# Attention scores in four row groups of the PE array: two heads per group in place of eight heads over all rows

## The chip, the cores and the metric

One core of a Trainium2 chip runs the whole kernel. The metric is device time in microseconds, from the start to the end of one execution. Three executions of the kernel before took 331.69, 332.37 and 332.95 us; the median is 332.37 us. Engines are named as in the profile: PE (matrix multiply), PEld (its weight loads), DVE (vector), ACT (scalar, activation), POOL (GpSimd), SP (the engine that issues most loads).

## The reference

One block of a gated cross-attention model on x of shape (2, 1024, 256), all in fp32, with a context of 77 rows per batch:

```
xn  = layernorm(x)                      # no gain, no bias
Q   = xn @ wq.T + bq                    # 16 heads of 16
K,V = ctx @ wk.T + bk, ctx @ wv.T + bv  # 77 keys per batch
s   = Q_h K_h^T / 4, masked: causal (key > query) and padded keys to -inf
x   = x + tanh(g_x) * (softmax(s) V @ wo.T + bo)
xt  = layernorm(x)
e   = argmax(xt @ Wr + br), gate = max softmax of the same
x   = x + tanh(g_f) * gate * expert_e(layernorm(xt))   # 8 experts, 256 -> 1024 -> 256, relu
```

With 77 keys and 1024 queries the causal mask bites only in the first 128 queries of each batch.

## The kernel before

The 2048 query rows are 16 tiles of 128 rows, 8 per batch. A short start loads and transposes the weights (`weight`, L1257: four 128x128 PE transposes into one PSUM bank, then an ACT copy), projects K for both batches, and builds `Kbd`. For each half m of the 256 model columns, eight heads of 16 columns lie on the 128 partitions, and `Kbd[:, b, m]` is block-diagonal: partition p holds the key values of its own head in that head's 77 columns and zero in the other seven heads' columns, 8 x 77 = 616 columns. DVE makes it for batch 0 (`key_blocks`, L788) and POOL for batch 1 in tile 3 (L410); both multiply by a constant mask of block positions (`bdm`).

A tile then goes through these steps, on the engines named. `query` (L1276): PE projects Q transposed, half m = 0 into bank A and half m = 1 into bank T0; ACT adds the bias and writes `QT` (L505, signal act_Q after each half). `scores(i, m)` (L1285): QT half m is the stationary operand (128 rows x 128 queries), Kbd the moving one, in two matmuls of 308 columns (four heads each), one PSUM bank each; in the first tile of a batch a bf16 matmul with an identity adds the mask bias to each bank. The signal pe_S rises after each half. DVE takes the maximum over each head's 77 keys (`smax`, L795), subtracts it and writes the probabilities' buffer `Pb` (`ssub`, L801); ACT takes exp in place (L513). PE transposes Pb in ten chunks in three groups (`transpose_P`, L1307), ACT copies each group to `PT` (`copy_PT`, L518), and PE multiplies with the block form of V in ten matmuls of 51 columns (`attend`, L1331). DVE divides by the row sums (`norm`), PE transposes the result (`transpose_O`, L1346), ACT copies it to `OT`, PE projects it (`project`, L1356) and DVE adds it to x.

The order of the work on every engine is written out by hand, and tiles overlap in it. In the pass of tile n PE runs: scores(n, 0), transpose_O(n-2), scores(n, 1), project(n-2), transposes of P(n-1) in groups 0 and 1, transposes for the layernorms of tiles n+1 and n-3, group 2 of P(n-1), attend(n-1), query(n+1), and the router's logits (`route`) of tile n-3 (L1434 to L1490). ACT runs: copy of OT(n-2), exp(n, 0), copies of PT(n-1), exp(n, 1), the writes of finished rows, and the two QT halves of tile n+1 (L582 to L614). DVE runs: maximum and subtraction of half 0, maximum of half 1, residual of tile n-2, subtraction of half 1, layernorm statistics, router, norm(n-1) (L1007 to L1055). Engines wait for each other by counting semaphores only.

After the tiles, rows are sorted by expert, written to a scratch tensor, gathered in groups of 128 rows of one expert, and the expert layers run over 16 or more such groups (L1546, L1567). That stage takes about half of the time and is not touched.

Of the kernel before, what the change touches and what calls it, by code (L numbers as in the profile page):

```python
# [10 lines left out]
ALU = mybir.AluOpType  # L11
# [3 lines left out]
B, S, D = 2, 1024, 256  # L15
H, DH = 16, 16
LK = 77
# [11 lines left out]
ROUND = 1.5 * 2.0 ** 30  # L29

CONST_COLS = [
    ("ident", 128), ("bdm", 8), ("causal", LK),
    ("e8", 8), ("before", 64), ("k128", 24), ("upto", 64), ("iota128", 128),
    ("pcol", 1), ("p32", 1), ("t1", NT), ("mhalf", 1),
]
# [23 lines left out]
def flamingo(nc, x, ctx_in, mask, g_x, g_f, wq, bq, wk, bk, wv, bv, wo, bo,  # L59
# [5 lines left out]
    with ExitStack() as ctx:  # L65
# [5 lines left out]
        def sbt(name, shape, dt=F32):  # L71

            return sb(name, shape, dt, tiles_only)
# [30 lines left out]
        bias0 = sbt("bias0", [128, B, LK], BF16)  # L104
        identb = sbt("identb", [128, 128], BF16)
# [6 lines left out]
        QT = sbt("QT", [128, 2, 128])  # L112
# [7 lines left out]
        xh = sbt("xh", [128, 2, D])  # L120
        Lg = sbt("Lg", [128, 2, 4, E])
        oh = sbt("oh", [128, NT, E], BF16)
        Kbd = sbt("Kbd", [128, B, 2, 8 * LK])

        iotab = sbt("iotab", [128, 128], BF16)
        ohr = Pb[:, 0, :].bitcast(BF16)[:, 0:NT * 128].rearrange("p (i r) -> p i r", r=128)
# [13 lines left out]
        wr4 = {n: stage("W1", 512).rearrange("p (k d) -> p k d", k=2) for n in ("wk", "wq", "wv", "wo")}  # L140
# [8 lines left out]
        KT = stage("W2", 2 * LK).rearrange("p (m k) -> p m k", m=2)  # L149
        CV = stage("W2", 2 * B * LK).rearrange("p (k b n) -> p k b n", k=2, b=B)  # L150
        vnat = stage("W2", B * H * 17, LK).rearrange("p (b h w) -> p b h w", b=B, w=17)
        brow = stage("W2", 128, 4)
# [5 lines left out]
        def cv(name):  # L158
            a, b_ = CONST_AT[name]
            return cst[:, a:b_]  # L160

        ident = cv("ident")


        pS = ctx.enter_context(nc.psum_tensor("pS", [128, 4, 512], F32))
# [6 lines left out]
        d = {n: sem(f"d_{n}") for n in LOADS}  # L172
# [26 lines left out]
        bank = {"A": pA[:, :], "B": pB[:, :], "S0": pS[:, 0, :], "S1": pS[:, 2, :], "T0": pT[:, 0, :],  # L199
                "T1": pT[:, 1, :]}  # L200
        pctx = pA[:, 0:320].rearrange("p (k n) -> p k n", k=2)[:, :, 0:B * LK]
        blocks = cv("bdm").unsqueeze(2).broadcast_to([128, 8, LK])
        b96_rows = (slice(0, 128), slice(64, 128), slice(64, 128), slice(96, 128), slice(96, 128))

        nth_high, nth_left = {}, {}
# [120 lines left out]
        def _(e):  # L326
# [50 lines left out]
                e.tensor_tensor(W2p[1][c][:, :], W2s[:, bass.ds(r_expert * 2048 + 512 * c, 512)], W2p[0][c][:, :],  # L377
                                ALU.subtract).then_inc(g["pool_W2l"], 1)

            e.dma_start(brow[0:2, :], bq.rearrange("(k p) -> k p", p=128)).then_inc(d["bq"], 16)  # L380
            e.dma_start(brow[2:4, :], bk.rearrange("(k p) -> k p", p=128)).then_inc(d["bk"], 16)
            e.dma_start(bvb, bv.partition_broadcast(128)).then_inc(d["bv"], 16)
            e.wait_ge(d["cst"], 16)
            rstd1(0)
# [10 lines left out]
            for n in range(NT):  # L395
                if n >= 2:
                    rstd2(n - 2)
                if n == 0:
                    e.wait_ge(d["bo"], 16)
                    e.wait_ge(g["act_tg"], 1)  # L400
                    e.tensor_scalar(bob[:, :], bob[:, :], tg[:, 0:1], None, ALU.mult).then_inc(g["pool_bo"], 1)
                    rstd1(2)
                    e.wait_ge(g["pool_bo"], 1)
                    x_plus_bias(0)
                    x_plus_bias(1)
                    e.tensor_copy(iotab[:, :], cv("iota128")).then_inc(g["pool_iota"], 1)
                    e.memset(pay[:, :, 513:PW], 0.0).then_inc(g["pool_pad"], 1)
                    e.wait_ge(d["up"], 16)
                    e.tensor_copy(upperb[:, :], upper).then_inc(g["pool_up"], 1)
                if n == 3:  # L410
                    for m in range(2):
                        e.wait_ge(g["act_KT"], m + 1)
                        e.tensor_tensor(Kbd[:, 1, m, :].rearrange("p (j k) -> p j k", j=8),
                                        KT[:, m, :].unsqueeze(1).broadcast_to([128, 8, LK]), blocks,
                                        ALU.mult).then_inc(g["pool_Kbd"], 1)
                if n + 3 < NT:
                    rstd1(n + 3)
                if n + 2 < NT:
                    x_plus_bias(n + 2)
                if n == 4:  # L420
                    e.wait_ge(g["pool_pad"], 1)
                if n >= 4:
                    store_row(n - 4)
# [65 lines left out]
        def _(e):  # L489
# [15 lines left out]
            def query(i):  # L505
                for m in range(2):
                    e.wait_ge(g["pe_Q"], 2 * i + m + 1)
                    if i:
                        e.wait_ge(g["pe_S"], 2 * (i - 1) + m + 1)
                    e.activation(QT[:, m, :], (pA, bank["T0"])[m][:, 0:128], ACT.Identity,  # L510
                                 bias=bqc[:, m:m + 1]).then_inc(g["act_Q"], 1)

# [248 lines left out]
        def _(e):  # L761
# [25 lines left out]

            def key_blocks(m):  # L788
                e.wait_ge(g["pe_K"], m + 1)
                e.scalar_tensor_tensor(out=Kbd[:, 0, m, :].rearrange("p (j k) -> p j k", j=8),  # L790
                                       in0=pS[:, 3 * m, 0:LK].unsqueeze(1).broadcast_to([128, 8, LK]),
                                       scalar=bkc[:, m:m + 1], in1=blocks, op0=ALU.add,
                                       op1=ALU.mult).then_inc(g["dve_Kbd"], 1)

            def smax(i, m):  # L795
                e.wait_ge(g["pe_S"], 2 * i + m + 1)
                e.tensor_reduce(mx[:, i % 2, 8 * m:8 * m + 8].rearrange("p (n h) -> p n h", n=2), heads(m), AX.X,  # L797
                                ALU.max).then_inc(g["dve_own"], 1)
                return own.up()
# [447 lines left out]
        def _(e):  # L1247
# [5 lines left out]
            def transpose(o, i):  # L1253
                n = i.shape[0]
                return e.transpose(o, i, ident[0:n, 0:n])  # L1255

            def weight(n, bk_):  # L1257

                e.wait_ge(d[n], 16)
                for k in range(2):  # L1260
                    for m in range(2):
                        t = transpose(bank[bk_][:, 256 * k + 128 * m:256 * k + 128 * m + 128],
                                      wr4[n][:, m, 128 * k:128 * k + 128])
                t.then_inc(g["pe_wT"], 1)

            def transpose_x(i):
# [15 lines left out]
                                     stop=(k == 1))  # L1282
                    t.then_inc(g["pe_Q"], 1)

            def scores(i, m):  # L1285
                b, first = i // TPB, i % TPB == 0
                e.wait_ge(g["act_Q"], 2 * i + m + 1)
                if i:
                    e.wait_ge(g["dve_Sm"], 2 * (i - 1) + m + 1)
                if first and m == 0:  # L1290
                    if b:
                        e.wait_ge(g["pool_Kbd"], 2)
                    else:
                        e.wait_ge(g["pool_id"], 1)
                        e.wait_ge(g["act_KT"], 1)
                    e.wait_ge(g["dve_bias0"], b + 1)
                if i == 0 and m == 1:
                    e.wait_ge(g["act_wT"], 3)
                for n in range(2):
                    o = pS[:, 2 * m + n, 0:308]  # L1300
                    t = e.matmul(o, QT[:, m, :], Kbd[:, b, m, 308 * n:308 * n + 308], start=True, stop=not first)  # L1301
                    if first:
                        t = e.matmul(o.rearrange("p (h k) -> p h k", h=4), identb[:, :],
                                     bias0[:, b, :].unsqueeze(1).broadcast_to([128, 4, LK]), start=False, stop=True)
                t.then_inc(g["pe_S"], 1)

            def transpose_P(i, grp):  # L1307
# [124 lines left out]
            e.wait_ge(g["dve_bcol"], 1)  # L1432
            weight("wv", "S1")
            for n in range(NT):  # L1434
                scores(n, 0)
                if n >= 2:
                    transpose_O(n - 2)
                scores(n, 1)
                if n >= 2:
                    project(n - 2)  # L1440
                if n == 1:
                    e.wait_ge(d["sel"], 16)
# [161 lines left out]
def constants():  # L1604
    import numpy as np
    c = np.zeros((128, CONST_W), np.float32)
    p = np.arange(128)

    def put(name, v):
        a, b_ = CONST_AT[name]  # L1610
        c[:, a:b_] = v
    put("ident", np.eye(128))
    put("bdm", (p[:, None] // 16) == np.arange(8)[None, :])
    bm = np.zeros((128, NC, 3, 17))
    sel = np.zeros((128, NC * 179 + 128), np.float32)
    for ch in range(NC):
        for r in range(128):
            row = 128 * ch + r
            if row < HK:
                bm[r, ch, row // LK - chunk_head(ch), :] = 1  # L1620
                sel[row % LK, row] = 1
    sel[:, NC * 128:NC * 179] = bm.reshape(128, -1)
    sel[:, NC * 179:] = p[:, None] < p[None, :]
    put("causal", np.arange(LK)[None, :] > p[:, None])
    put("e8", np.arange(8)[None, :] / 8)
    put("before", (np.arange(8)[None, :] < np.arange(8)[:, None]).reshape(1, 64))
    put("k128", 128 * np.arange(24)[None, :])
    put("upto", (np.arange(8)[None, :] <= np.arange(8)[:, None]).reshape(1, 64))
    put("iota128", p[None, :])
    put("p32", np.where((p % 32 < 8) & (p // 32 != 1), p % 32, -1)[:, None])  # L1630
    put("pcol", p[:, None])
    put("t1", 128 * np.arange(NT)[None, :])
    put("mhalf", -0.5)
    return c, sel
# [24 lines left out]
```

## Time and profile before

| what | value |
|---|---|
| median of 3 runs | 332.37 us |
| profiled execution, its own time | 332.82 us |
| its span, first to last instruction | 330.9 us |
| mean granted clock of PE | 0.957 of full |
| PE busy | 301.2 us (91%) |
| DVE busy | 212.5 us (64%) |
| ACT busy | 181.8 us (55%) |
| POOL busy | 135.9 us (41%) |
| score matmuls (L1301) | 128 passes, 40.2 us busy |

Busy times count an instruction from its start to its end as the profile models it. Matmuls are pipelined, so on PE the end of one lies behind the start of the next, and sums of durations exceed the time that passes; starts and the pieces of the chain are the safer reading. An fp32 matmul appears as two matmul records, each with its own weight load.

### The profile page before, as it was taken

Reading aid. Unit: us, or ns where it says so; the run is one execution under the profiler, and the core shown is the slowest. Engines: PE = TensorE matmul, PEld = TensorE weight load, DVE = VectorE, ACT = ScalarE, POOL = GpSimd, SP = SyncE. Lnnn points to the kernel's source line nnn. Section 1 sums busy time; section 2 is a strip of 40 time slices with the busy share of each in tenths; the row PEclk is TensorE's granted clock in tenths of the full one; section 3 lists DMA queues with packets and bytes.
Section 4 is the critical chain, followed back from the end, with each engine's and each line's share of the span. In section 5 each row is a group of like instructions: output and inputs, shape, how many; then the busy total and the mean of one; then the engine's idle time right before and its main releaser. Section 6 shows DMA issues by size and latency. Waiting matters only on the chain.

```text
span 330.9 us, 7543 instructions
## 1 busy us (share of the span) xinstructions
PE 301.2 (91%) x2348; PEld 276.5 (84%) x2348; DVE 212.5 (64%) x666; ACT 181.8 (55%) x485; POOL 135.9 (41%) x247
## 2 busy tenths in 40 slices
PE   6899999999999999998456999999999999999960
PEld 2569898889899999988325999999999999999960
DVE  4588789989888887777773774345446653344640
ACT  2325567776666666663425875554358743555540
POOL 2444446544444544422635166332234832332250
PEclk9799999999999999999856999999999999999995
DMA  6999990000004444441214102222112121112100
GB/s 172 274 320 378 374 320 8 32 33 34 33 34 161 160 161 159 162 160 43 89 44 120 33 7 66 67 57 70 56 48 62 34 82 51 62 54 77 53 17 5
DMA packets 19890, 34.52 MB, mean 104 GB/s; under 512 B 2564, under 2 KB 14656, under 8 KB 19845
## 3 DMA queue, kind: packets, MB, share of 16 engines
q1 hardware_dynamic: 15509, 21.29, 19.7%
q0 software_dynamic: 4192, 12.62, 12.3%
q8 instruction: 21, 0.34, 0.4%
q14 instruction: 24, 0.20, 0.2%
q10 hardware_dynamic: 144, 0.07, 0.1%
HBM read 27.61 MB, written 6.88 MB: 104 GB/s over the span
## 4 chain that ended last, share of the span: by engine, by line
PE 73%; DVE 7%; issue 5%; ACT 4%; DMA 3%; POOL 3%; POOLq 1%; SPq 1%; DVEq 0%; ACTq 0%
PE pS L1546 21%; PE pB L1567 15%; PE pS L1301 9%; PE pB L1342 9%; PE pT L1255 5%; PE pA L1255 4%; PE pB L1367 3%; DMA W1s<-in_L_xattn_wq_dram 2%; PE pA L1281 2%; PE pT L1281 1%; DMA zin<-rows_dram,idxg 1%; PE pT L1376 1%; POOL W2p L377 1%; DVE Pb L805 1%; DVE mx L797 1%
## 5 line engine op out<-in xcount | busy, mean ns | idle before, releaser
L1546 PE MATMUL pS<-znf,W1c 128*128 128x128 f32 x672 | 83.9, 280 | 0.0
L1546 PEld LDWEIGHTS pS<-znf,W1c 128*128 128x128 f32 x672 | 80.8, 197 | 0.0
L1567 PE MATMUL pB<-W2p,hT 128*128 128x256 f32 x480 | 62.7, 286 | 0.3
L1567 PEld LDWEIGHTS pB<-W2p,hT 128*128 128x128 f32 x480 | 58.7, 191 | 0.9 <-POOL W2p L377 0.7
L1179 DVE TENSOR_SCALAR hA<-pS,b1s 128x128 f32<-128x128 f32 x84 | 23.7, 344 | 54.6 <-PE pS L1546 31.6
L371 POOL DMA_INDIRECT out_dram<-yo,idxs x20 | 21.5, 1074 | 72.7 <-DVE yo L1193 54.9
L681 ACT ACTIVATE hA<-pS,b1s 128x128 f32<-128x128 f32 x84 | 24.0, 368 | 44.4 <-PE pS L1546 38.6
L1301 PE MATMUL pS<-Kbd,QT 128*128 128x308 f32 x128 | 40.2, 433 | 1.9 <-ACT QT L510 1.0
L1342 PE MATMUL pB<-VB,PT 128*128 128x51 f32 (+1 forms) x320 | 37.3, 272 | 0.0
L1342 PEld LDWEIGHTS pB<-VB,PT 128*128 128x128 f32 (+1 forms) x320 | 37.0, 192 | 0.0
L516 ACT ACTIVATE Pb<-Pb 128x616 f32<-128x616 f32 x32 | 23.2, 724 | 24.2 <-DVE Pb L805 24.2
L797 DVE TENSOR_REDUCE mx<-pS 128x8 f32<-128x616 f32 x32 | 25.4, 794 | 11.1 <-PE pS L1301 10.1
L692 ACT ACTIVATE hT<-hA 128x512 fp32r<-128x512 f32 x42 | 27.1, 645 | 8.1 <-DVE hA L1179 7.7
L365 POOL DMA_INDIRECT zin<-rows_dram,idxg x23 | 23.5, 1020 | 17.4 <-issue 13.3
L1301 PEld LDWEIGHTS pS<-Kbd,QT 128*128 128x128 f32 x128 | 21.7, 190 | 7.5 <-ACT QT L510 2.6
L1186 DVE TENSOR_TENSOR hT<-hA,hT 128x512 fp32r<-128x512 f32 x42 | 27.9, 703 | 0.1
L805 DVE TENSOR_TENSOR Pb<-pS,mx 128x616 f32<-128x616 f32 x32 | 25.4, 795 | 1.9 <-DVE mx L797 0.5
L343 POOL TENSOR_SCALAR mv<-mv 128x1 f32<-128x1 f32 x16 | 3.5, 221 | 53.9 <-DVE mv L833 53.8
L1255 PE MATMUL pT<-cst,Pb 128*128 128x128 f32 (+1 forms) x160 | 23.5, 277 | 0.6 <-DVE Lg L847 0.4
L1255 PEld LDWEIGHTS pT<-cst,Pb 128*128 128x128 f32 (+1 forms) x160 | 17.7, 139 | 3.6 <-issue 0.8
L524 ACT ACTIVATE PT<-pT 128x512 f32<-128x512 f32 x32 | 17.6, 594 | 4.0 <-PE pT L1255 2.9
L673 ACT ACTIVATE znf<-pA,bcol 128x128 f32<-128x128 f32 x44 | 18.1, 477 | 2.0 <-PE pA L1255 2.0
(198 smaller groups left out, 497.1 us busy)
## 6 DMA issues: line engine op xcount, KB each, us to landing
W1s<-in_L_ffn_W_dram SPq DMA_DIRECT2D x8, 1024.0 KB, 9.7
W2s<-in_L_ffn_W_dram SPq DMA_DIRECT2D x8, 1024.0 KB, 11.2
rows_dram<-pay POOLq DMA_DIRECT2D x16, 260.0 KB, 2.6
xs<-in_x_dram SPq DMA_DIRECT2D x3, 512.0 KB, 7.7
W2s<-in_sel_dram SPq DMA_DIRECT2D x1, 385.0 KB
zin<-rows_dram,idxg POOLq DMA_INDIRECT x23, 3.7
out_dram<-yo,idxs POOLq DMA_INDIRECT x20
W1s<-in_L_xattn_wk_dram SPq DMA_DIRECT2D x1, 256.0 KB, 3.2
```

The source lines that it names most:

```text
L365: e.indirect_dma_start(zin[s % NZ][:, :], None, scratch, bass.IndirectOffsetOnAxis(ap=idxg[:, s:s + 1], axis=0)).then_inc(gsem[s % NZ], 16)
L681: e.activation(hA[2 * (s % 2)][:, 128 * c:128 * c + 128], pS[:, 2 * (s % 2), 128 * c:128 * c + 128], ACT.Relu, bias=b1s[:, c, s:s + 1]).th ...
L692: e.activation(hT[s % 2][0][:, 512 * n:512 * n + 512], hA[2 * (s % 2) + n][:, :], ACT.Copy).then_inc(g["act_hT"], 1)
L797: e.tensor_reduce(mx[:, i % 2, 8 * m:8 * m + 8].rearrange("p (n h) -> p n h", n=2), heads(m), AX.X, ALU.max).then_inc(g["dve_own"], 1)
L805: e.tensor_tensor(Pb[:, i % 2, 616 * m:616 * m + 616].rearrange("p (n h k) -> p n h k", n=2, h=4), heads(m), mx[:, i % 2, 8 * m:8 * m + 8] ...
L1179: e.tensor_scalar(hA[2 * (s % 2) + 1][:, 128 * c:128 * c + 128], pS[:, 2 * (s % 2) + 1, 128 * c:128 * c + 128], b1s[:, 4 + c, s:s + 1], 0. ...
L1186: e.tensor_tensor(lo, hA[2 * (s % 2) + n][:, :], hi, ALU.subtract).then_inc(g["dve_hT"], 1)
L1255: return e.transpose(o, i, ident[0:n, 0:n])
L1301: t = e.matmul(o, QT[:, m, :], Kbd[:, b, m, 308 * n:308 * n + 308], start=True, stop=not first)
L1342: t = e.matmul(pB[:, 17 * h0:17 * h0 + 51], PT[0:n, i % 2, c, :], VB[0:n, b, c, :], start=(c == 0), stop=(c == NC - 1), skip_group_check=True)
L1546: t = e.matmul(pS[:, 2 * (s % 2) + n, 128 * c:128 * c + 128], W1c[k][n][:, 128 * c:128 * c + 128], znf[s % 2][:, 128 * k:128 * k + 128], s ...
L1567: t = e.matmul(o, hT[s % 2][a][:, 128 * c:128 * c + 128], W2p[b_][c // 2][:, D * (c % 2):D * (c % 2) + D], start=False, stop=(c == 7 and a ...
```

## The change

The 16 heads are laid out differently, and the scores are computed in 32-row groups of the array. The rows of Q and K are permuted (in the transposes of wq and wk, and in the loads of bq and bk) so that half m holds, in partitions 32r to 32r+31, the two heads 4r + 2m and 4r + 2m + 1. Kbd then needs only 2 x 77 = 154 columns per half: which two heads they are depends on the partition's group. The scores of a tile are eight matmuls of 32 rows x 154 columns, group r writing to PSUM bank r, first the columns of m = 0 and then those of m = 1, so each bank holds four heads in the old order. All eight are one call, with one signal pe_S at its end; it waits for both halves of QT and, for the bank space, for both subtractions of the tile before. In PE's order transpose_O(n-2) and project(n-2) follow that call directly. What DVE and ACT do with the scores keeps its shapes.

```diff
-        Kbd = sbt("Kbd", [128, B, 2, 8 * LK])
+        Kbd = sbt("Kbd", [128, B, 2, 2 * LK])
...
-            e.dma_start(brow[0:2, :], bq.rearrange("(k p) -> k p", p=128)).then_inc(d["bq"], 16)
-            e.dma_start(brow[2:4, :], bk.rearrange("(k p) -> k p", p=128)).then_inc(d["bk"], 16)
+            for lo, v, n in ((0, bq, "bq"), (2, bk, "bk")):
+                e.dma_start(brow[lo:lo + 2, :].rearrange("m (r x) -> m r x", r=4),
+                            v.rearrange("(r m x) -> m r x", r=4, m=2)).then_inc(d[n], 16)
...
                     if i:
-                        e.wait_ge(g["pe_S"], 2 * (i - 1) + m + 1)
+                        e.wait_ge(g["pe_S"], i)
...
             def smax(i, m):
-                e.wait_ge(g["pe_S"], 2 * i + m + 1)
+                e.wait_ge(g["pe_S"], i + 1)
...
                 for k in range(2):
+                    o = bank[bk_][:, 256 * k:256 * k + 256]
+                    by_head = o.rearrange("p (m r x) -> p r m x", m=2, r=4)
                     for m in range(2):
-                        t = transpose(bank[bk_][:, 256 * k + 128 * m:256 * k + 128 * m + 128],
-                                      wr4[n][:, m, 128 * k:128 * k + 128])
+                        t = transpose(by_head[:, 2 * m:2 * m + 2, :, :] if n in ("wq", "wk")
+                                      else o[:, 128 * m:128 * m + 128], wr4[n][:, m, 128 * k:128 * k + 128])
...
-            def scores(i, m):
+            def scores(i):
                 b, first = i // TPB, i % TPB == 0
-                e.wait_ge(g["act_Q"], 2 * i + m + 1)
+                e.wait_ge(g["act_Q"], 2 * i + 2)
                 if i:
-                    e.wait_ge(g["dve_Sm"], 2 * (i - 1) + m + 1)
+                    e.wait_ge(g["dve_Sm"], 2 * i)
...
-                        e.wait_ge(g["act_KT"], 1)
+                        e.wait_ge(g["act_KT"], 2)
+                        e.wait_ge(g["act_wT"], 3)
...
-                for n in range(2):
-                    o = pS[:, 2 * m + n, 0:308]
-                    t = e.matmul(o, QT[:, m, :], Kbd[:, b, m, 308 * n:308 * n + 308], start=True, stop=not first)
-                    if first:
-                        t = e.matmul(o.rearrange("p (h k) -> p h k", h=4), identb[:, :],
-                                     bias0[:, b, :].unsqueeze(1).broadcast_to([128, 4, LK]), start=False, stop=True)
+                for m in range(2):
+                    for r in range(4):
+                        rows = slice(32 * r, 32 * r + 32)
+                        t = e.matmul(pS[:, r, 154 * m:154 * m + 154], QT[rows, m, :], Kbd[rows, b, m, :],
+                                     start=(m == 0), stop=(m == 1 and not first), skip_group_check=True)
+                if first:
+                    for r in range(4):
+                        t = e.matmul(pS[:, r, 0:308].rearrange("p (h k) -> p h k", h=4), identb[:, :],
+                                     bias0[:, b, :].unsqueeze(1).broadcast_to([128, 4, LK]), start=False, stop=True,
+                                     skip_group_check=True)
                 t.then_inc(g["pe_S"], 1)
...
             for n in range(NT):
-                scores(n, 0)
+                scores(n)
                 if n >= 2:
                     transpose_O(n - 2)
-                scores(n, 1)
-                if n >= 2:
                     project(n - 2)
```

## Rows read from the trace of the kernel before

**Rows 1.** Busy time by stretch: us, then PE, PEld, DVE, ACT, POOL (instructions), clock, DMA
```profile
91.90:141.70 49.80, 49.80 (x362) 44.97 (x362) 41.00 (x129) 32.25 (x86) 23.17 (x57) 1.00 0.40 139
```
**Rows 2.** The page's chain that ended last, by line, shares of the span
```profile
PE pS L1546 21%; PE pB L1567 15%; PE pS L1301 9%; PE pB L1342 9%; PE pT L1255 5%; PE pA L1255 4%; PE pB L1367 3%; DMA W1s<-in_L_xattn_wq_dram 2%; PE pA L1281 2%; PE pT L1281 1%; DMA zin<-rows_dram,idxg 1%; PE pT L1376 1%; POOL W2p L377 1%; DVE Pb L805 1%; DVE mx L797 1%
```
**Rows 3.** The chain in order of time, tile 11: start us, us, what
```profile
109.81 0.22 PE pA L1255 x2
110.03 1.04 PE pS L1301 x4
111.07 0.86 PE pB L1367 x4
...
113.49 2.17 PE pB L1342 x20
```
**Rows 4.** Timeline of PE, tile 11: start us, us, engine line op out<-in xcount
```profile
108.53 1.28 PE L1301 MATMUL pS<-Kbd,QT 128*128 128x308 f32 x4
109.65 0.38 PE L1255 MATMUL pA<-cst,On 128*128 128x128 f32 x2
...
110.90 1.03 PE L1367 MATMUL pB<-woT,OT 128*128 128x256 f32 x4
111.77 1.04 PE L1255 MATMUL pT<-cst,Pb 128*128 128x128 f32 x8
...
116.82 0.76 PE L1301 MATMUL pS<-Kbd,QT 128*128 128x308 f32 x2
```
**Rows 5.** Timeline of ACT, then of DVE, tile 11
```profile
108.36 0.37 ACT L510 ACTIVATE QT<-pT,bcol 128x128 f32<-128x128 f32 x1
110.06 0.39 ACT L534 ACTIVATE OT<-pA 128x256 f32<-128x256 f32 x1 [1.33 <-PE pA L1255]
111.58 0.72 ACT L516 ACTIVATE Pb<-Pb 128x616 f32<-128x616 f32 x1 [1.13 <-DVE Pb L805]
112.40 1.09 ACT L524 ACTIVATE PT<-pT 128x512 f32<-128x512 f32 x2
...
109.85 0.80 DVE L797 TENSOR_REDUCE mx<-pS 128x8 f32<-128x616 f32 x1 [0.68 <-PE pS L1301]
110.75 0.80 DVE L805 TENSOR_TENSOR Pb<-pS,mx 128x616 f32<-128x616 f32 x1
```
**Rows 6.** Timeline, tile 15
```profile
145.12 0.72 ACT L516 ACTIVATE Pb<-Pb 128x616 f32<-128x616 f32 x1 [1.49 <-DVE Pb L805]
...
145.75 1.07 ACT L524 ACTIVATE PT<-pT 128x512 f32<-128x512 f32 x2
...
146.38 0.44 PE L1255 MATMUL pT<-cst,Pb 128*128 128x128 f32 x2 [0.17 <-ACT PT L524]
```
**Rows 7.** Timeline of ACT, then of PE, start of tile 6
```profile
65.26 0.37 ACT L510 ACTIVATE QT<-pA,bcol 128x128 f32<-128x128 f32 x1
...
65.68 1.30 PE L1301 MATMUL pS<-Kbd,QT 128*128 128x308 f32 x4 [0.54 <-ACT QT L510]
```
**Rows 8.** Timeline of PE after the last tile: transpose and projection with nothing between
```profile
153.69 0.40 PE L1255 MATMUL pA<-cst,On 128*128 128x128 f32 x2
...
154.56 1.13 PE L1367 MATMUL pS<-woT,OT 128*128 128x256 f32 x4 [0.47 <-ACT OT L534]
```
**Rows 9.** Timeline of the start and of tiles 0 and 1
```profile
8.99 1.11 PE L1255 MATMUL pT<-cst,W1s 128*128 128x128 f32 x4 [2.60 <-DMA W1s<-in_L_xattn_wq_dram]
...
13.09 1.63 DVE L790 SCALAR_TENSOR_TENSOR Kbd<-pS,bcol,cst 128x616 f32<-128x616 f32 x2 [0.89 <-PE pS L1427]
...
14.98 0.59 ACT L502 ACTIVATE W1s<-pS 128x512 f32<-128x512 f32 x1
15.55 0.76 PE L1301 MATMUL pS<-Kbd,QT 128*128 128x308 f32 x2 [0.74 <-DVE bias L785]
17.29 0.80 DVE L797 TENSOR_REDUCE mx<-pS 128x8 f32<-128x616 f32 x1
...
24.09 0.78 DVE L797 TENSOR_REDUCE mx<-pS 128x8 f32<-128x616 f32 x1
```

More of the change, by code:

```diff
@@ L31 @@
 CONST_COLS = [
-    ("ident", 128), ("bdm", 8), ("causal", LK),
+    ("ident", 128), ("pair", 2), ("causal", LK),
     ("e8", 8), ("before", 64), ("k128", 24), ("upto", 64), ("iota128", 128),
@@ L201, in flamingo @@
         pctx = pA[:, 0:320].rearrange("p (k n) -> p k n", k=2)[:, :, 0:B * LK]
-        blocks = cv("bdm").unsqueeze(2).broadcast_to([128, 8, LK])
+        pairs = cv("pair").unsqueeze(2).broadcast_to([128, 2, LK])
         b96_rows = (slice(0, 128), slice(64, 128), slice(64, 128), slice(96, 128), slice(96, 128))
@@ L412, in _ @@
                         e.wait_ge(g["act_KT"], m + 1)
-                        e.tensor_tensor(Kbd[:, 1, m, :].rearrange("p (j k) -> p j k", j=8),
-                                        KT[:, m, :].unsqueeze(1).broadcast_to([128, 8, LK]), blocks,
+                        e.tensor_tensor(Kbd[:, 1, m, :].rearrange("p (j k) -> p j k", j=2),
+                                        KT[:, m, :].unsqueeze(1).broadcast_to([128, 2, LK]), pairs,
                                         ALU.mult).then_inc(g["pool_Kbd"], 1)
@@ L789, in key_blocks @@
                 e.wait_ge(g["pe_K"], m + 1)
-                e.scalar_tensor_tensor(out=Kbd[:, 0, m, :].rearrange("p (j k) -> p j k", j=8),
-                                       in0=pS[:, 3 * m, 0:LK].unsqueeze(1).broadcast_to([128, 8, LK]),
-                                       scalar=bkc[:, m:m + 1], in1=blocks, op0=ALU.add,
+                e.scalar_tensor_tensor(out=Kbd[:, 0, m, :].rearrange("p (j k) -> p j k", j=2),
+                                       in0=pS[:, 3 * m, 0:LK].unsqueeze(1).broadcast_to([128, 2, LK]),
+                                       scalar=bkc[:, m:m + 1], in1=pairs, op0=ALU.add,
                                        op1=ALU.mult).then_inc(g["dve_Kbd"], 1)
             def smax(i, m):
-                e.wait_ge(g["pe_S"], 2 * i + m + 1)
+                e.wait_ge(g["pe_S"], i + 1)
                 e.tensor_reduce(mx[:, i % 2, 8 * m:8 * m + 8].rearrange("p (n h) -> p n h", n=2), heads(m), AX.X,
@@ L1283, in query @@
                     t.then_inc(g["pe_Q"], 1)
-            def scores(i, m):
+            def scores(i):
                 b, first = i // TPB, i % TPB == 0
-                e.wait_ge(g["act_Q"], 2 * i + m + 1)
+                e.wait_ge(g["act_Q"], 2 * i + 2)
                 if i:
-                    e.wait_ge(g["dve_Sm"], 2 * (i - 1) + m + 1)
-                if first and m == 0:
+                    e.wait_ge(g["dve_Sm"], 2 * i)
+                if first:
                     if b:
@@ L1294, in scores @@
                         e.wait_ge(g["pool_id"], 1)
-                        e.wait_ge(g["act_KT"], 1)
+                        e.wait_ge(g["act_KT"], 2)
+                        e.wait_ge(g["act_wT"], 3)
                     e.wait_ge(g["dve_bias0"], b + 1)
-                if i == 0 and m == 1:
-                    e.wait_ge(g["act_wT"], 3)
-                for n in range(2):
-                    o = pS[:, 2 * m + n, 0:308]
-                    t = e.matmul(o, QT[:, m, :], Kbd[:, b, m, 308 * n:308 * n + 308], start=True, stop=not first)
-                    if first:
-                        t = e.matmul(o.rearrange("p (h k) -> p h k", h=4), identb[:, :],
-                                     bias0[:, b, :].unsqueeze(1).broadcast_to([128, 4, LK]), start=False, stop=True)
+                for m in range(2):
[3 more added lines that the diff above has]
+                                     start=(m == 0), stop=(m == 1 and not first), skip_group_check=True)
+                if first:
+                    for r in range(4):
+                        t = e.matmul(pS[:, r, 0:308].rearrange("p (h k) -> p h k", h=4), identb[:, :],
+                                     bias0[:, b, :].unsqueeze(1).broadcast_to([128, 4, LK]), start=False, stop=True,
+                                     skip_group_check=True)
                 t.then_inc(g["pe_S"], 1)
@@ L1612, in constants @@
     put("ident", np.eye(128))
-    put("bdm", (p[:, None] // 16) == np.arange(8)[None, :])
+    put("pair", (p[:, None] % 32 // 16) == np.arange(2)[None, :])
     bm = np.zeros((128, NC, 3, 17))
```

## The prediction

> **What bounds the kernel now.** I read the busy shares by stage first. From 91.9 to 141.7 us PE is busy 49.80 of 49.80 us and DVE 41.00 [rows 1]. The chain that ended last gives the score line L1301 9% of the span; the largest shares, L1546 and L1567, are the expert layers, which this change doesn't touch [rows 2]. So the score matmuls are on the path. Next the chain in order of time for tile 11: the pieces are all PE's, one after another. The first score call takes 1.12 us (108.53 to the transposes at 109.65) and the second 1.04, in a period of 8.29 (108.53 to 116.82) [rows 3, 4]. So PE is the bound from tile 9 on.
>
> Then I asked how much air the other engines have, because a shorter PE helps only until the next chain is late. That chain goes round as well: scores, DVE maximum (L797) and subtraction (L805), ACT exp (L516), and only behind the exp, in ACT's order, the copy of the transposed probabilities (L524) for which PE waits before its last transposes and L1342. In tile 11: score start 108.53, maximum 109.85, subtraction 110.75, exp 111.58, copy 112.40 [rows 4, 5]. The exp was not what the copy waited for there: in tile 15 the copy starts 0.63 us after the exp (145.12, 145.75), in tile 11 0.82 after, so this chain has 0.19 us of air in 3.87. Tile 15 also shows what happens when the air is gone: copy at 145.75, PE starts its last transposes at 146.38 with "ACT PT L524" as releaser [rows 6]. In tile 6, with more on ACT, the score matmul itself waits for QT from ACT (65.68) [rows 7]. Two chains are nearly equally long, and the change shortens one of them and may lengthen the other.
>
> **The change, part by part.**
>
> *Column time of the scores: nothing saved in itself.* Each fp32 matmul shows as two passes, each with a weight load. Before, 4 matmuls of 308 columns are 8 passes; 1.04 us for 4 of them is 0.26 each [rows 3]. L1367 gives the same per column (0.86 us for 4 passes of 256). After, 8 matmuls of 154 columns are 16 passes of 0.13: again 2.08 us. Weight loads double, from 8 to 16. L1342 gives their price where the moving side is short: 20 passes of 51 columns in 2.17 us, 0.109 each [rows 3]. All gain must come from row groups working at once, of which no row here has an example. I call the PE time of a tile's scores X and bound it:
> - nothing at once: 16 x 0.13 = 2.08;
> - loads one after another, matmuls overlapped: 16 x 0.109 + 0.13 = 1.87;
> - both overlapped, matmuls starting in program order. The order is r0 first pass, r0 second pass, r1 first pass, ... The two passes of one group share its rows and can't overlap, while the second pass of one group can lie beside the first of the next: 8 x 0.13 + 0.13 = 1.17;
> - all four groups free of each other: 4 rounds x 0.13 = 0.52.
>
> I take 1.17. Loads already run ahead of matmuls here (0.109 under a 0.26 pass), so I expect overlap, but two passes behind each other in one group block the queue.
>
> The Trainium skill bears on this twice. "TensorE: Matmul & The Clock Gate", Part 3, says four row tiles start about 4 ns apart, which would put X near 0.55, the last bound. The same part says matmuls start and end strictly in program order, which leads to 1.17 for this order of passes. No run here shows either. "TensorEngine Tiling (Array Packing)", Key Properties, says a change of tiling mode drains the engine; by that the transposes behind the scores would start later, by up to the 0.24 us by which four passes outlast their 4 x 0.26 (1.28 shown at 108.53 [rows 4]).
>
> *Both halves of Q first.* The scores now wait for act_Q of both halves. In tile 11 the second QT ends 108.36 + 0.37 = 108.73 [rows 5]; a score starts about 0.05 after its QT (tile 6: 65.26 + 0.37 = 65.63, score 65.68 [rows 7]). So 108.78 in place of 108.53: +0.25. Behind this wait on PE stand transpose_O, project and the transposes of the probabilities. The other waits, dve_Sm of the tile before and pe_S before overwriting QT, were met long ago.
>
> *One signal in place of two.* DVE's first maximum waited for half of the scores and now waits for all. Before, it began 1.32 us after the score start, 0.29 more than the 4 x 0.26 of PE time. After, 0.25 + X + 0.29. The rest of that chain keeps its shapes: 0.90 to the subtraction, 0.83 to the exp, at least 0.63 to the copy. The copy starts at 0.25 + X + 0.29 + 2.36 = 2.90 + X, against 3.87 before. **A tile changes by X - 0.97**: +0.20 at X = 1.17.
>
> *The cover of transpose_O's copy is gone.* The second score call stood between transpose_O and project. Before: transpose 109.65, OT copy 110.06 (0.39), project 110.90, never late. Where nothing covers it the tail shows the price: transpose 153.69, project 154.56, PE idle with "ACT OT L534" as releaser: 0.87 for two transposes that take 0.22, so 0.65 us of new idle [rows 3 to 5, 8]. On PE the copy of the probabilities may then start at 0.25 + X + 0.87 + 0.87 (project) + 0.63 (transposes to copy, 111.77 to 112.40) = 2.62 + X. That is 0.28 earlier than by DVE's chain, so the gap is hidden behind DVE and ACT, and a drain under 0.28 with it. Without that cover the gap would cost its 0.65 per tile.
>
> *Start.* Kbd on DVE shrinks from 616 to 154 columns twice: most of 1.63 us at 13.09, off the path. The scores also wait for ACT's third weight copy, 14.98 + 0.59 = 15.57; an earlier Kbd lets ACT's first KT begin up to 0.5 earlier, but QT and wv bound that, so I give it 0.1: score start 15.5, as before (15.55). The first maximum, at 17.29, then waits for all: 15.5 + 1.17 + four bias passes at 0.13 + 0.1 for their first load + 0.29 = 17.58, +0.3. DVE is the path there, so it counts. In tile 1 the maximum at 24.09 follows with no idle time before it, so DVE was late there and not the scores, and nothing changes [rows 9]. The strided outputs of the wq and wk transposes: wk's lie before wq arrives (8.99); wq's 1.11 us is on the path, so between 0 and +0.5 if the strides halve their rate; I take 0, since only the order within the row changes. The bias loads on POOL's queue are cut into eight pieces each in place of two; PE transposes them ahead of wq, and at 8.99 it had waited 2.60 us for wq, so up to that a later landing is covered [rows 9]. Kbd on POOL for the second batch shrinks, and POOL is 23.17 of 49.80 us busy [rows 1].
>
> *Sum.* Tiles 2 to 15: 14 x 0.20 = 2.8. Tile 0: 0.3. Together +3.1 us. The profiled execution took 332.82 (span 330.9 and 1.9 around it) and gives 335.9; the median, 332.37, lies 0.45 under it and gives 335.5. Uncertain inside this case: X by 0.1 (1.4 us), waits by 0.05 a tile (0.7), wq's transposes 0.5, so 333 to 338.
>
> **The rivals.** "Same" is within 0.5%, 1.7 us, about what this kernel's measurement can tell from no change.
> - *Groups wholly independent (faster).* X = 0.52: 14 x (0.52 - 0.97) = -6.3, tile 0 -0.35: 325.7. It decides the sign from X = 0.97 down. PE by its own waits would be at 2.62 + 0.52 = 3.14, DVE's chain at 3.42, so nothing else catches the gain. For: four banks and four groups don't touch each other. Against: the two passes per group stand together in the order.
> - *Loads don't overlap.* X = 1.87: 14 x 0.90 = 12.6, tile 0 +1.0: 346.0. For: L1342 runs at exactly the load's pace, never faster. Against: those loads all fill the same rows.
> - *It doesn't do what it says.* The groups run one after another, X = 2.08: 14 x 1.11 = 15.5, tile 0 +1.2: 349.1. For: no row shows groups at once.
>
> **How the numbers follow.** Program-order overlap 0.36, independent groups 0.28, loads in series 0.25, nothing at once 0.11. Likeliest: 335.5, its own range 333 to 338. The range 326 to 348 takes in the first rival but its last 0.3 us and the second with 2 us of air, and leaves most of the third out. Faster: 0.26 of the independent case and 0.02 of the likeliest, 0.28. Within: 0.02 and 0.07, 0.09. Slower: 0.27 + 0.25 + 0.11 = 0.63.
>
> **What the profile after would show.** Score starts 8.5 us apart in tiles 9 to 14 (8.29 before), 7.9 for the first rival, 9.2 and 9.4 for the others. Score starts sitting behind the second QT. The first maximum 1.17 + 0.29 after the score start. PE idle about 0.65 before project with OT as releaser, and before the last transposes with PT as releaser. I am wrong if the first maximum comes less than 1.2 us after the score start (the groups are freer than the order allows), if PE never waits for PT (the DVE chain is not the bound), or if transpose_O starts more than 0.28 late after the last score pass (the drain decides).

## The result: faster, by about one per cent

The changed kernel took 328.63 us (median of 4 runs, 326.49 to 331.83) beside 332.42 before: ratio 0.9855, interval 0.9826 to 0.9883. Timed once more beside the kernel before, it took 329.83 against 332.58 (medians): ratio 0.9891, interval 0.9855 to 0.9926. Runs at the slow end of its scatter, one in each series, are left out of the ratios, and not of the medians. The forecast was 335.5, slower. The time lay inside its range, on the other side of no change.

The chain that ended last, changed kernel, by engine and by line (before: [rows 2]). The score line, now L1306, falls from 9% to 3%, and ACT and DVE have 20% of the chain (11% before):

```profile
PE 61%; DVE 11%; ACT 9%; issue 7%; DMA 3%; POOL 3%; POOLq 1%; SPq 1%; DVEq 0%; ACTq 0%
PE pS L1552 22%; PE pB L1573 15%; PE pB L1350 6%; PE pA L1257 4%; PE pT L1257 4%; PE pS L1306 3%; PE pB L1375 3%; DVE mx L799 2%; DVE Pb L807 2%; DMA cst<-in_consts_dram 2%; ACT QT L512 2%; DMA zin<-rows_dram,idxg 1%; ACT PT L526 1%; PE pA L1285 1%; ACT Pb L518 1%
```

Timeline of PE, tile 11 (before: [rows 4]). Score starts are 7.92 us apart (8.29 before), and PE idles 0.47 us before project:

```profile
106.80 0.81 PE L1306 MATMUL pS<-Kbd,QT 32*128 32x154 f32 x16
107.53 0.44 PE L1257 MATMUL pA<-cst,On 128*128 128x128 f32 x2
108.45 1.13 PE L1375 MATMUL pB<-woT,OT 128*128 128x256 f32 x4 [0.47 <-ACT OT L536]
109.42 1.04 PE L1257 MATMUL pT<-cst,Pb 128*128 128x128 f32 x8
...
114.72 0.81 PE L1306 MATMUL pS<-Kbd,QT 32*128 32x154 f32 x16
```

ACT and DVE in the same tile (before: [rows 5]):

```profile
106.38 0.37 ACT L512 ACTIVATE QT<-pT,bcol 128x128 f32<-128x128 f32 x1
108.01 0.38 ACT L536 ACTIVATE OT<-pA 128x256 f32<-128x256 f32 x1 [1.27 <-PE pA L1257]
109.41 0.72 ACT L518 ACTIVATE Pb<-Pb 128x616 f32<-128x616 f32 x1 [1.01 <-DVE Pb L807]
110.05 1.08 ACT L526 ACTIVATE PT<-pT 128x512 f32<-128x512 f32 x2
...
107.67 0.80 DVE L799 TENSOR_REDUCE mx<-pS 128x8 f32<-128x616 f32 x1 [0.32 <-PE pS L1306]
108.58 0.80 DVE L807 TENSOR_TENSOR Pb<-pS,mx 128x616 f32<-128x616 f32 x1
```

Sixteen passes last 0.81 us from the first start to the last end, and the first maximum comes 0.87 after the start. Taking off the 0.29 that the prediction put between PE's time and the maximum, X is 0.58. A stretch of 0.02 us at the start of the same call, PE and its loads, shows four passes and four loads under way together:

```profile
106.80 0.41 PE L1306 MATMUL pS<-Kbd,QT 32*128 32x154 f32 x4
106.80 0.20 PEld L1306 LDWEIGHTS pS<-Kbd,QT 32*128 32x128 f32 x4 [0.20 <-ACT QT L512]
```

Where the time went, by stage: from tile 2's score start to tile 15's it took 105.49 us (33.02 to 138.51) against 109.98 (31.73 to 141.71), so -4.5. From tile 0's score start to tile 2's it took 17.50 against 16.18, so +1.3. From tile 15's score start to the first expert matmul (L1546, now L1552) 35.98 against 36.26, so -0.3. Together -3.5. The profiled runs differ by 5.0 (332.82, 327.83); the other 1.5 lies behind the start of the last expert matmul, 9.5 us to the end against 11.0. That is not the row groups' doing: with them and without, this stretch took 9.4 to 9.6 us in ten of the profiles and 10.9 to 11.3 in four (9.5 with the full rows of the first experiment, 10.9 with the row groups and the fill below). The +1.3 is new, in rows of the changed kernel (start of the program, PE, then the clock as the third figure from the right):

```profile
21.58 0.81 PE L1306 MATMUL pS<-Kbd,QT 32*128 32x154 f32 x16 [0.29 <-ACT QT L512]
24.03 1.33 PE L1454 MATMUL pT<-W2s 77*128 77x102 f32 x10 [1.64 <-DVE bcol L1053]
25.20 2.02 PE L1454 MATMUL pB<-W2s 77*128 77x102 f32 x10
...
33.02 0.81 PE L1306 MATMUL pS<-Kbd,QT 32*128 32x154 f32 x16
...
138.51 0.81 PE L1306 MATMUL pS<-Kbd,QT 32*128 32x154 f32 x16
```
```profile
24.00:27.00 3.00, 2.97 (x20) 3.00 (x21) 2.69 (x4) 0.72 (x1) 2.39 (x7) 0.76 1.09 363
27.00:29.00 2.00, 2.00 (x12) 2.00 (x11) 1.72 (x4) 0.64 (x2) 0.00 (x0) 0.51 1.04 404
```

The same in the kernel before:

```profile
24.32 1.33 PE L1448 MATMUL pT<-W2s 77*128 77x102 f32 x10 [0.37 <-DVE bcol L1051]
25.48 1.28 PE L1448 MATMUL pB<-W2s 77*128 77x102 f32 x10
...
31.73 1.20 PE L1301 MATMUL pS<-Kbd,QT 128*128 128x308 f32 x4
...
141.71 1.28 PE L1301 MATMUL pS<-Kbd,QT 128*128 128x308 f32 x4
```
```profile
27.00:29.00 2.00, 2.00 (x19) 1.75 (x17) 1.92 (x7) 1.76 (x6) 0.00 (x0) 1.00 1.01 388
```

The shorter score call leaves PE idle for 1.64 us in tile 1, where it waits for DVE (0.37 before), and then the granted clock goes to its lower level, 1.2 GHz. Ten matmuls of one shape take 2.02 us just after ten of the same shape took 1.33; before, 1.33 and 1.28. Before, the clock was 1.00 in both stretches.

### The profile page after: what moved, and what is told of

It reads as the page before. It is cut to its first block, busy times and chain, and to the rows that moved or that the text cites. A ratio compares the mean times of both kernels' runs of the same rounds, so it can differ in the third digit from the quotient of the medians.

```text
span 325.8 us, 7783 instructions
## 1 busy us (share of the span) xinstructions
PE 285.8 (88%) x2476; PEld 264.3 (81%) x2476; DVE 211.3 (65%) x666; ACT 180.7 (55%) x485; POOL 134.3 (41%) x247
## 4 chain that ended last, share of the span: by engine, by line
PE 61%; DVE 11%; ACT 9%; issue 7%; DMA 3%; POOL 3%; POOLq 1%; SPq 1%; DVEq 0%; ACTq 0%
PE pS L1552 22%; PE pB L1573 15%; PE pB L1350 6%; PE pA L1257 4%; PE pT L1257 4%; PE pS L1306 3%; PE pB L1375 3%; DVE mx L799 2%; DVE Pb L807 2%; DMA cst<-in_consts_dram 2%; ACT QT L512 2%; DMA zin<-rows_dram,idxg 1%; ACT PT L526 1%; PE pA L1285 1%; ACT Pb L518 1%
## 5 line engine op out<-in xcount | busy, mean ns | idle before, releaser
L1552 PE MATMUL pS<-znf,W1c 128*128 128x128 f32 x672 | 83.8, 279 | 0.0
L1552 PEld LDWEIGHTS pS<-znf,W1c 128*128 128x128 f32 x672 | 80.7, 197 | 0.0
L1257 PE MATMUL pT<-cst,Pb 128*128 128x128 f32 (+1 forms) x160 | 24.2, 284 | 0.8 <-DVE Lg L849 0.4
L1375 PE MATMUL pB<-woT,OT 128*128 128x256 f32 x56 | 15.8, 405 | 6.6 <-ACT OT L536 6.6
L1257 PEld LDWEIGHTS pT<-cst,Pb 128*128 128x128 f32 (+1 forms) x160 | 18.6, 144 | 3.6 <-ACT PT L526 0.9
L1375 PEld LDWEIGHTS pB<-woT,OT 128*128 128x128 f32 x56 | 9.5, 189 | 10.7 <-ACT OT L536 10.0
## 6 DMA issues: line engine op xcount, KB each, us to landing
W2s<-in_L_ffn_W_dram SPq DMA_DIRECT2D x8, 1024.0 KB, 11.3
```

The lines of the kernel that those rows point to most:

```text
L1375: t = e.matmul(pr_bank(i), OT[:, k, :], wT["wo"][:, k, :], start=(k == 0), stop=(k == 1))
L1552: t = e.matmul(pS[:, 2 * (s % 2) + n, 128 * c:128 * c + 128], W1c[k][n][:, 128 * c:128 * c + 128], znf[s % 2][:, 128 * k:128 * k + 128], s ...
```

## The experiments

**The price of the merged call.** Full 128-row matmuls as before, with the changed kernel's order, waits and single signal (shown against the changed kernel, in part):

```diff
-                        t = e.matmul(pS[:, r, 154 * m:154 * m + 154], QT[rows, m, :], Kbd[rows, b, m, :], ...
+                        t = e.matmul(o, QT[:, m, :], Kbd[:, b, m, 308 * n:308 * n + 308], ...
```

> The kernel before with its full 128-row score matmuls (8 passes of 308 columns, 2.08 us of PE time), but with the order, the waits and the one signal of the changed kernel. It prices the reorder alone. The prediction's rule (period 8.29 + X - 0.97, the way through DVE and ACT) gives score starts 9.4 us apart in tiles 9 to 14 and about 349 us. Rival: PE's own way alone counts (scores, idle before project, project, transposes): 9.1 apart and about 345 us. Second rival: the order costs nothing, 8.3 to 8.5 apart and 332 to 335 us.

349.68 us, ratio 1.0485 (1.0442 to 1.0528), score starts 9.40 apart. The prediction's rule gave 9.40 and 349. So the reorder costs 1.1 us a tile at X = 2.08. Of the two ways to the copy the one through DVE and ACT ends last, but only by 0.10 us, as the rows show: the copy starts 0.62 behind the exp, and the transposes that it copies, 0.63 ahead of it in other tiles, started 0.73 ahead here:

```profile
111.50 2.34 PE L1301 MATMUL pS<-Kbd,QT 128*128 128x308 f32 x8
113.88 0.80 DVE L797 TENSOR_REDUCE mx<-pS 128x8 f32<-128x616 f32 x1 [1.97 <-PE pS L1301]
...
115.50 1.04 PE L1255 MATMUL pT<-cst,Pb 128*128 128x128 f32 x8
115.61 0.72 ACT L516 ACTIVATE Pb<-Pb 128x616 f32<-128x616 f32 x1 [1.14 <-DVE Pb L805]
...
116.23 1.07 ACT L524 ACTIVATE PT<-pT 128x512 f32<-128x512 f32 x2
```

**Does program order hold a group back?**

```diff
-                for m in range(2):
-                    for r in range(4):
+                for r in range(4):
+                    for m in range(2):
```

> The same eight score matmuls, issued group by group (both halves of group 0, then of group 1, ...) in place of half by half. After the change the 16 passes of a tile took 0.58 us of PE time, four at once. Theory A (each row group works off its own matmuls, whatever stands before them in program order): the same 0.81 us from the first score pass to the end of the last, score starts 7.92 us apart in tiles 9 to 14. Rival B (a matmul may not start before the one ahead of it has started, and the half-by-half order is what hid that): two matmuls of one group block the next group, starts at 0, 0.26, 0.26, 0.52, ... 1.04, so 1.30 us of PE time, 1.5 us first to last, score starts 8.5 to 8.7 apart. Rival C (B for single passes): 1.7 us of PE time, score starts about 9.0 apart.

0.83 us, 7.95 apart: theory A. For matmuls of different groups it made no difference which of the two orders they stood in.

```profile
109.45 0.83 PE L1306 MATMUL pS<-Kbd,QT 32*128 32x154 f32 x16
117.40 0.83 PE L1306 MATMUL pS<-Kbd,QT 32*128 32x154 f32 x16
```

**Is it the distinct groups?**

```diff
-                        rows = slice(32 * r, 32 * r + 32)
+                        rows = slice(0, 32)
```

> The changed kernel with all eight score matmuls of a tile reading rows 0 to 31 (QT and Kbd of group 0; the scores of the other groups' heads are left out, group 0's stand in their place). Same count, same shapes, same banks, but one row group. If distinct row groups are what lets four passes run at once: the 16 passes follow each other, 16 x 0.13 = 2.08 us of PE time, about 2.3 from first start to last end, score starts 9.4 us apart in tiles 9 to 14. Rival: the narrow form is cheap in itself (32 rows, or distinct banks): 0.8 us as before and 7.9 apart.

2.36 us from first to last: one group works in series, and narrowness alone gives nothing. From tile 3 on its tiles are 9.5 to 12.5 us apart and the kernel takes 386.09 us, more than the rule says: the granted clock fell again and again though PE was busy (stretch from 90 us: 45.34 of 48 us, clock 0.78):

```profile
109.34 2.36 PE L1306 MATMUL pS<-Kbd,QT 32*128 32x154 f32 x16
90.00:138.00 48.00, 45.34 (x278) 40.87 (x277) 30.36 (x93) 24.49 (x63) 16.41 (x40) 0.78 0.13 45
```

With two groups, by turns (`rows = slice(32 * (r % 2), 32 * (r % 2) + 32)`):

> As e9_one_group, with groups 0 and 1 by turns (groups 2 and 3 left out, 0 and 1 in their place). If each group works off its own passes: 8 x 0.13 = 1.04 us of PE time, 1.25 to 1.35 from first start to last end; the rule 8.29 + X - 0.97 gives 8.4 us from score to score. Rival: four at once or none, then 0.8 or 2.3 us.

1.32 us, and 8.44 apart where the clock was up (8.4 forecast); 10.1 in the tiles where it fell (0.93 over the stretch). So 2.36, 1.32, 0.81 for one, two and four groups: the time halves with each doubling, but for 0.3 us that stays.

```profile
98.58 1.32 PE L1306 MATMUL pS<-Kbd,QT 32*128 32x154 f32 x16
107.02 1.32 PE L1306 MATMUL pS<-Kbd,QT 32*128 32x154 f32 x16
```

**What sets the pace after the change?** In tile 11 the copy at 110.05 is ready by two ways at once: through DVE and ACT, exp at 109.41 and 0.64 on; through PE, transposes at 109.42 and 0.63 on. To tell whether both bind, one move on PE and one on ACT, each alone and both:

```diff
+                if n:
+                    transpose_P(n - 1, 0)          # PE: ahead of project
                 if n >= 2:
                     project(n - 2)
...
-                    transpose_P(n - 1, 0)          # PE: behind project
...
+                if n:
+                    copy_PT(n - 1, 0)              # ACT: ahead of exp
                 exp(n, 0)
...
-                    copy_PT(n - 1, 0)              # ACT: behind exp
```

> The move on PE alone (first four transposes of P(n-1) before project), ACT's order as in the changed kernel. If DVE and ACT's way binds by itself: score starts 7.9 us apart in tiles 9 to 14, as without the move. If PE's way alone was the bound: 7.4 to 7.6.

> The move on ACT alone (copy of the first P(n-1) chunks before exp(n, 0)), PE's order as in the changed kernel. If PE's way binds by itself: 7.9 us apart in tiles 9 to 14. If DVE and ACT's way alone was the bound: 7.4 to 7.6.

> The changed kernel with two moves: PE transposes the first four chunks of P(n-1) between transpose_O(n-2) and project(n-2), where PE waits 0.47 us for OT, and ACT copies them before exp(n, 0) and not behind it. After the change two ways to that copy are equally long: through PE (scores, idle, project, transposes: 3.25 us from the score start) and through DVE and ACT (maximum, subtraction, exp: 3.25). Theory: both bind, and with both moved the period falls from 7.92 to about 7.4 us in tiles 9 to 14 (PE's work plus the rest of the two waits), 5 to 7 us less than the changed kernel in all. Rival: another engine (DVE, 41.2 of 47.6 us busy there) is the bound as well, and the period stays above 7.8.

7.89, 7.95 (from tile 10 on) and, from tile 10 on, 7.58 (7.92 without a move). In these tiles neither alone does anything, both together take 0.34 off, a little less than expected. With PE's move alone PE waits for the copy, which stands behind the exp; with ACT's move alone the copy waits for PE (a row of each):

```profile
106.33 0.44 PE L1257 MATMUL pT<-cst,Pb 128*128 128x128 f32 x2 [0.22 <-ACT PT L526]
```
```profile
116.48 0.60 ACT L526 ACTIVATE PT<-pT 128x512 f32<-128x512 f32 x1 [1.66 <-PE pT L1258]
```

From tile 3 to tile 10 ACT's move alone makes the tiles longer, 8.5 to 9.2 us in place of 7.9 to 8.7, and its one run took 333.08. With both moves the first transposes fill PE's wait for OT, and the copy no longer stands behind the exp:

```profile
110.88 0.81 PE L1307 MATMUL pS<-Kbd,QT 32*128 32x154 f32 x16
111.62 0.44 PE L1258 MATMUL pA<-cst,On 128*128 128x128 f32 x2
111.89 0.60 PE L1258 MATMUL pT<-cst,Pb 128*128 128x128 f32 x4
112.09 0.38 ACT L536 ACTIVATE OT<-pA 128x256 f32<-128x256 f32 x1 [1.26 <-PE pA L1258]
112.53 1.13 PE L1376 MATMUL pB<-woT,OT 128*128 128x256 f32 x4
112.53 0.60 ACT L526 ACTIVATE PT<-pT 128x512 f32<-128x512 f32 x1
...
113.50 0.72 ACT L518 ACTIVATE Pb<-Pb 128x616 f32<-128x616 f32 x1 [0.37 <-DVE Pb L808]
```

The whole time with both is no better all the same (329.51, ratio 0.9885, 0.9853 to 0.9916). From tile 3's score start to tile 9's, where the scores of either kernel wait for QT from ACT, the moves gain 0.6 us, from tile 9's to tile 15's 1.8; and in the profile tile 0 to tile 2 took 21.45 us (17.50 in the changed kernel's first profile), with the clock down past 33 us. The same two moves on the kernel before:

> The kernel before (full-row scores in two calls) with the two moves of e4_probs_ahead. Theory: before the change PE's own work sets the period in tiles 9 to 14 and has no gap before project, so the moves give nothing there: 8.25 to 8.3 us from score to score; the room that the moves used was made by the row groups. Rival: the copy's order was a bound of the kernel before as well, then 8.0 or less.

8.26: next to nothing. The row groups made the room.

**The wait for the second half of Q.**

```diff
-                e.wait_ge(g["act_Q"], 2 * i + 2)
+                e.wait_ge(g["act_Q"], 2 * i + 1)
...
                 for m in range(2):
+                    e.wait_ge(g["act_Q"], 2 * i + m + 1)
                     for r in range(4):
```

> The changed kernel, with the four matmuls of half 0 waiting for the first QT only, and those of half 1 for the second. If the wait for the second QT is on the path, as forecast at +0.25 us a tile, the first maximum comes 0.15 to 0.25 earlier behind the second QT, score to score 7.7 us in tiles 9 to 14 in place of 7.92, and 2 to 3.5 us less in all. Rival: that wait is hidden (the time is set by another way round), then 7.92 stays and the time is that of the changed kernel.

7.75 apart from tile 10 on. The wait was on the path, worth 0.17 of the 0.25 forecast. The second half shows no wait of its own: the 16 passes take 0.81 us as without the split. The scores now follow PE's matmuls for the router's logits (L1385) at once, so PE's own order sets their start:

```profile
112.73 0.51 PE L1385 MATMUL pT<-wrs,XX 128*128 128x8 f32 x4
112.93 0.37 ACT L512 ACTIVATE QT<-pT,bcol 128x128 f32<-128x128 f32 x1
113.17 0.81 PE L1307 MATMUL pS<-Kbd,QT 32*128 32x154 f32 x16
```

In the whole time a gain over the changed kernel is not shown: its six runs lie between 324.45 and 331.93, with a median of 330.42. In the profiled one, the longest of them, the clock was still at 0.50 from 29 to 33 us.

**The clock at the start.**

```diff
                 if n == 1:
+                    warm(7, bank["T1"])
                     e.wait_ge(d["sel"], 16)
```

> The changed kernel with seven bf16 matmuls of ones (about 1.5 us, into a free PSUM bank) between the scores of tile 1 and what follows. There the changed kernel left PE idle 1.64 us and the granted clock read 0.51 from 27 to 29 us (1.00 before the change). Theory: the idle time brings the clock down and this costs 1.3 to 1.5 us at the start; then the clock is 1.00 from 24 to 29 us, tile 2's scores start near 31.6 us in place of 33.02, and the ratio to the kernel before falls by about 0.004. Rival: the clock falls for another reason (the 32-row matmuls count for less), then it reads about 0.5 there as well and nothing is gained.

The clock stays at 1.00 from 24 to 29 us, and tile 0 to tile 2 takes 16.11 us (17.50 without, 16.18 before the change):

```profile
27.00:29.00 2.00, 2.00 (x19) 1.71 (x18) 1.97 (x5) 1.39 (x4) 0.15 (x1) 1.00 1.05 400
16.18 0.81 PE L1306 MATMUL pS<-Kbd,QT 32*128 32x154 f32 x16 [0.93 <-ACT W1s L504]
32.29 0.81 PE L1306 MATMUL pS<-Kbd,QT 32*128 32x154 f32 x16
```

So filling the idle time keeps the clock up. That the idle time alone brings it down is not shown, since the fill adds full-row matmuls as well. The rival (32-row matmuls count for less) is not ruled out either: with all scores in one row group (the third experiment) PE had no wait for DVE in tile 1, and the clock fell all the same, while with full rows in one call (the first), where the scores of tile 1 start at 23.90 in place of 23.86 and last 2.34 in place of 2.36, it stayed up. Full rows, then one group:

```profile
27.00:29.00 2.00, 2.00 (x21) 2.00 (x19) 1.97 (x4) 0.72 (x1) 1.71 (x5) 1.00 1.04 407
```
```profile
27.00:29.00 2.00, 2.00 (x14) 2.00 (x13) 1.97 (x4) 0.72 (x1) 1.67 (x4) 0.61 1.02 389
```

So the clock can fall there without that wait, where few rows are at work; whether the wait alone is enough, with full-row scores, was not run. In the whole time (327.5, ratio 0.9836, 0.9801 to 0.9871) the gain of the fill is within the intervals' overlap and not shown. The unaltered changed kernel, timed once more:

> The changed kernel once more, unaltered, timed beside the kernel before. Theory: PE's idle time in tile 1 brings the clock down there in every run, for a length that varies, so the runs scatter by 3 to 5 us (326 to 332) where the kernel before scatters by 2; the fast ones lie near 328, and the clock reads about 0.5 after 25 us in the profile. Rival: the low clock at the start was an accident of single runs, then 1.00 there.

It scattered from 327.63 to 333.22 (the kernel before from 331.76 to 333.96), and the clock was down again, for longer; tile 0 to tile 2 took 19.05 us:

```profile
27.00:29.00 2.00, 2.00 (x12) 2.00 (x11) 1.06 (x2) 0.41 (x1) 0.72 (x2) 0.50 1.02 396
16.75 0.81 PE L1306 MATMUL pS<-Kbd,QT 32*128 32x154 f32 x16 [0.92 <-ACT W1s L504]
35.80 0.81 PE L1306 MATMUL pS<-Kbd,QT 32*128 32x154 f32 x16
```

The clock fell there in all seven profiles of four-group kernels without the fill (the changed kernel twice, and five versions of it), and stayed up in the two with it and in the three with full-row scores.

**All of it together:** the two moves, the split wait and the fill.

> The two moves, the split wait for Q and the fill of PE's idle time in tile 1, all on the changed kernel. If the gains are on one way round they add: period 7.1 to 7.3 us in tiles 9 to 14 and 1.4 us at the start, 317 to 321 us. If DVE becomes the bound: 7.3 to 7.5, and 321 to 324 us.

323.84 us, ratio 0.9709 (0.9681 to 0.9736), 7.4 us apart in tiles 10 to 14. It beats both kernels, and is slower than 317 to 321. The time is that of the second case, but its cause is not: in tiles 11 and 12 (103 to 118 us) every piece of the chain that ended last is PE's but for short issue times, and none is DVE's. Its shares there by line:

```profile
by line: PE pB L1352 31.3%; PE pB L1377 15.1%; PE pT L1258 14.6%; PE pA L1258 10.7%; PE pS L1308 9.8%; PE pA L1286 6.8%; PE pT L1286 6.0%; PE pT L1386 5.4%; issue 0.5%
```

Against the changed kernel's first profile it gains 1.6 us from tile 0 to tile 2 and 2.6 from tile 9 to tile 15, but only 1.2 from tile 3 to tile 9.

## Why the prediction was wrong

- *Column time, the choice of X.* This step failed. It took program-order overlap, X = 1.17; the trace shows 0.58, near the 0.52 of the rival "groups wholly independent". The argument was that the two passes of one group block the queue; the group-by-group order shows that they don't. Four row groups work off their passes at once: from first start to last end 0.81 us with four, 1.32 with two, 2.36 with one. The loads, of which the prediction had feared 0.109 each in series, run four at once. The Trainium skill, "TensorE: Matmul & The Clock Gate", Part 3, has both rules that were weighed: row tiles starting some 4 ns apart agrees with four starts within 0.02 us here; strict program order of starts and ends would have made the group-by-group call longer, and 0.83 us for it speaks against that across groups.
- *The rule, a tile changes by X - 0.97.* Right. At X = 2.08 it gave 9.40, measured 9.40; for two groups 8.4, measured 8.44; at 0.58 it gives 7.90, measured 7.92. With X right the prediction's own sum gives 326.6, near the rival's 325.7, where 328.63 and 329.83 were measured.
- *Both halves of Q:* forecast +0.25. QT ends at 106.75 and the scores start at 106.80. Splitting the wait gave back 0.17, and then PE's own order sets the start. Right in kind, and nearly in size.
- *The cover of OT's copy.* The idle time came, 0.47 us with OT as releaser. It was forecast to hide with 0.28 to spare; the spare was zero, since transpose to project and project to transposes took 0.92 and 0.97 where 0.87 each was reckoned, and the transposes behind the scores started 0.15 late, less than the 0.28 at which the prediction would have put it down to a drain. PE never waited for PT in tiles 9 to 14, one of the signs of being wrong; yet the way through DVE and ACT was no shorter, since moving transposes into the gap was worth something only together with the move on ACT. So both ways bind.
- *Start.* Mis-sized: +0.3 for tile 0 and nothing for tile 1. The first maximum of tile 0 came at 17.00, where 17.58 was forecast: with 0.58 for X the same sum gives 16.99. The maximum in tile 1 did wait for DVE and not for the scores, as said. But PE then stood idle, and tile 0 to tile 2 took 1.3 us more than before in the first profile and 2.9 in the second, with the clock down; the prediction has no term for the clock. Beside the 4.5 that the tiles gain, that is a third in the one and two thirds in the other.
- *Rivals.* Loads in series (346.0) and nothing at once (349.1) are ruled out by X. The independent case had a chance of 0.28 where program order had 0.36; its 325.7 lacks the time lost at the start.

## What to carry to other kernels

Four row groups on four banks cut the PE time of these 32-row matmuls to nearly a quarter (2.08 to 0.58 us), in both orders of issue that were tried; whether it takes four banks was not tried. What the kernel gains is only what the next chain leaves, here 0.37 of 1.5 us a tile. When one call replaces two, price the cover that the second one gave and the signal that the first one gave early; if two ways tie, only moving both shows a gain. A shorter call can leave the array idle somewhere else, so look at the granted clock of every stretch after it.

## What was not expected of the hardware

Matmuls that use few rows of the array let the clock fall though PE is busy: with one row group at work in the scores the granted clock was 0.78 from 90 to 138 us, PE busy for 45.34 of 48 us; with two groups 0.93 over the same stretch; with four 1.00, and with the full rows in one call, whose scores take as long as the one group's, 1.00 as well (44.70 of 48 us). And once down at the start, how long it stays down differs: from 29 to 33 us it read 1.00 in the changed kernel's first profile, 0.64 in its second and 0.50 in the split wait's, where it fell a second time, in tile 6 (0.50 from 74 to 76 us, 9.7 us to the next scores). That fits the scatter of these kernels; the clock at the start of runs without a profile was not read.
